# Scores a slot earlier, later turns of the second norms, reordered gathers and a split turning of the first keys in a fused language-model tower

## The chip, the cores and the metric

The kernel runs as one program on one core of a Trainium2 chip. Its time is the device time of one execution, in microseconds (us). The core has four engines that compute side by side, each with its own instruction stream: TensorE (PE in the profile; its weight loads are PEld), VectorE (DVE), ScalarE (ACT) and GpSimd (POOL). SyncE (SP) here only issues DMAs. The engines wait for one another by semaphores. The kernel before took 1109.43 us (median of three runs, 1108.84 to 1109.99).

## The reference

32 sequences of 128 tokens with 192 features, all in fp32, go through four steps:

```python
# 1 embedding
emb = word_table[ids] + domain_table[dom] @ proj_w.T + proj_b + types + pos
h = layer_norm(emb) * ln_gamma + ln_beta
# 2 "magnitude" attention, 12 heads of 16 features, on layer_norm(h)
sr = (qr @ kr.T + qi @ ki.T) * scale
si = (qi @ kr.T - qr @ ki.T) * scale
h = h + softmax(sqrt(sr * sr + si * si)) @ v
# 3 causal attention, 12 heads, on layer_norm(layer_norm(h)) (two norms, one behind the other)
x = layer_norm(h); x = x + attention(ln1(x)) @ proj_w + proj_b
# 4 mixture of 8 experts on ln2(x): the 2 best of 8 per token, at most 1280 tokens an expert
x = x + moe(ln2(x));  return h + x
```

## The kernel before

The 32 sequences are eight groups of four. Each group passes through the magnitude attention in one pass (passes 0 to 7) and through the causal attention in another (passes 8 to 15); the experts follow, from about 756 us on. A pass has 16 slots, and TensorE, VectorE, ScalarE and GpSimd walk the same passes and slots in their own `one_pass` functions. The work is software pipelined: while the group of the pass has its scores made, the group before has its probabilities transposed and multiplied by the values, and the next group has its input normalised, transposed and projected. What an engine does in a slot beside scores are "fills" (`fills_of`): pieces such as `xT` (transposes of the normalised input xn), `proj` and `value` (projections to q, k and values), `probT` (transposes of the probabilities), `ctx`, `ctxT`, `out`, `zT` and `logits`. Each fill takes the next of three places in PSUM in turn (`PLACE`, `RING`), so the order of the fills is the order in which the places come free.

*Magnitude scores.* A group has 12 jobs (four sequences x three blocks of heads), one a slot, job j in slot j + `SCORE_SLOT`. TensorE's `scores` multiplies k by q, both halves of the complex product from 32 rows of k: the second half uses `k_signed`, the keys with real and imaginary parts exchanged and one sign changed. ScalarE squares (`squares`), VectorE adds the squares and takes row maxima (`maxima`), ScalarE takes roots and later exponentials. The exchange is made by DMAs: VectorE writes k and k_signed of a block after its projection (in slots 12, 12 and 13 of the pass before), and SyncE copies k_signed in eight DMAs a block (sixteen partitions each) into k. The job of block b in a group's first three jobs waits for `keys_turned[b]`. In group 0 SyncE waits for all three blocks and issues eight DMAs that carry all of them (`first_turned`). For groups 1 to 7 that is 24 DMAs each, 168 in all.

*Embedding.* GpSimd gathers word, place (position and type) and domain rows by indirect DMAs, four of each a group (`gather_step`), and takes a power for the scale of each norm (`embedding_norm`: the first power in slot 4; the second in slot 6, or 12 for groups 2 to 7). VectorE makes xn from the second.

*Causal passes.* For each of a group's four sequences, three slots apart, come in turn `ctx` (values product done), `ctxT` (transposed context), `out` (output projection), `scale` (power on GpSimd), `norm` (VectorE makes z, the second norm's result), `zT` (TensorE transposes z), `keep` (z stored) and `logits` (router). `LAGS` gives the slots, counted from the group's own pass plus 16; the last group has shorter ones in `LAST_LAGS`.

*The set-up.* Before pass 0 SyncE also loads inputs and weights; the first groups have earlier projections (`EARLY_PROJ`).

Of the kernel before, what the change touches and what calls it, by code (L numbers as in the profile page):

```python
# [31 lines left out]
BLOCKS = 3  # L32
# [15 lines left out]
RING = 3  # L48
SCORE_SLOT = {"mag": 2, "cau": 3}
EXP_SLOT = 4  # L50
MAG_PROJ = (12, 12, 13, 13, 14, 15)
MAG_VALUE = (10, 14)
# [32 lines left out]

LAGS = {"ctx": 5, "ctxT": 7, "out": 9, "scale": 10, "norm": 12, "zT": 13, "keep": 13, "logits": 15}
LAST_LAGS = {"ctx": 5, "ctxT": 6, "out": 8, "scale": 8, "norm": 10, "zT": 11, "keep": 11, "logits": 13}
# [74 lines left out]
def tower_kernel(nc, ids, word_table, domain_cols, pos_table, kind_rows, domain_w, mag_qk, mag_v,  # L162
                 causal_qk, causal_qk_b, causal_v, ln_cols, rows, out_w, gate_w, fc_w, fc_b, pj_w, pj_b, out):
    ctx = ExitStack()
    with ctx:
# [6 lines left out]
        def sem(name):  # L172
            return ctx.enter_context(nc.semaphore(name))
# [161 lines left out]
        keys_signed = sem("keys_signed")  # L335
        first_turned = sem("first_turned")
        keys_turned = [sem(f"keys_turned{b}") for b in range(BLOCKS)]
        sign_made = sem("sign_made")
# [75 lines left out]
        CONST = 10 * 16  # L414
        
        blk = ctx.enter_context(nc.Block())

# [8 lines left out]
        def _(sp):  # L426
# [45 lines left out]
            sp.dma_start(fc_bias[:, :, :], fc_b).then_inc(bias_loaded, 16)  # L472

            sp.wait_ge(keys_signed, BLOCKS)
            for quarter, part in product(range(4), range(2)):
                to, of = 32 * quarter + HEAD_DIM * part, 32 * quarter + HEAD_DIM * (1 - part)
                sp.dma_start(k_of[0][to:to + HEAD_DIM, :, 1, :, :].rearrange("p b s k -> p b (s k)"),
                             k_signed[of:of + HEAD_DIM, :, :]).then_inc(first_turned, 16)
            for g in range(1, GROUPS):
# [62 lines left out]
        def _(pool):  # L542
# [69 lines left out]
            def embedding_norm(p, g, slot):  # L612
                first, second = (4, 6) if g < 2 else (4, 12)
                if slot == first:
                    pool.wait_ge(mag.named("emb_moments"), g + 1)
                    power(g, moments[:, :, 1], rstd[:, 0, :], WORD_EPS, mag, "emb_rstd")
                elif slot == second:
                    pool.wait_ge(mag.named("x_moments"), g + 1)
                    power(g, moments[:, :, 1], rstd[:, 1, :], LN_EPS, mag, "x_rstd")
# [121 lines left out]
        def _(pe):  # L741
# [112 lines left out]
            def scores(number, j):  # L854
# [7 lines left out]
                if p is mag and j % 3 == j:  # L862

                    if g > 0:
                        pe.wait_ge(keys_turned[j], 8 * 16 * g)
                    else:
                        pe.wait_ge(first_turned, 8 * 16)
                for pair in range(2):
# [30 lines left out]
            def one_pass(p):  # L899
                now, ready = group_of(p, 0), group_of(p, -1)  # L900
                for slot in range(STEPS):
# [4 lines left out]
                    if now is not None and 0 <= slot - SCORE_SLOT[phase_of(now)[0].name] < JOBS:  # L906
                        scores(now, slot - SCORE_SLOT[phase_of(now)[0].name])
                    if ready is not None and 1 <= slot <= JOBS:
                        values_product(ready, slot - 1)
                    for n, f in fills:  # L910
                        fill(n, f)

            def domain_products():
# [117 lines left out]
        def _(act):  # L1031
# [95 lines left out]
            def expert_weights_high(e, u):  # L1127
                act.wait_ge(raw_loaded, 48 * e + 48)
                apart(act)
                sc.activation(fc_hi[:, u, :, :], raw_fc, ACT.Copy).then_inc(fc_high, 1)  # L1130

            def first_weights_high(quarter):

# [4 lines left out]
            def one_pass(p):  # L1138
                now, ready = group_of(p, 0), group_of(p, -1)
                for slot in range(STEPS):  # L1140
# [12 lines left out]
                    for n, f in fills:  # L1153
                        fill(n, f)
                    if ready is not None and slot >= 3 and slot % 3 == 0 and slot // 3 <= GROUP:
                        copy_ctx(*phase_of(ready), slot // 3 - 1)
# [84 lines left out]
        def _(dve):  # L1241
# [12 lines left out]
            def fill(number, fl):  # L1254
# [35 lines left out]
                elif kind == "proj" and p is mag and s < 3:  # L1290
# [4 lines left out]
                    if g == 1:  # L1295
                        dve.wait_ge(first_turned, 8 * 16)
                    elif g > 1:
                        dve.wait_ge(keys_turned[s], 8 * 16 * (g - 1))
# [490 lines left out]
```

## Time and profile before

| what | value |
|---|---|
| median of the runs | 1109.43 us (1108.84 to 1109.99) |
| profiled execution, its own time | 1110.32 us |
| its span | 1107.4 us |
| busy share of the span | PE 86%, PEld 65%, ACT 61%, DVE 60%, POOL 41% |
| granted TensorE clock in 40 slices of 27.7 us, tenths | 7668889989999999999999998656999999999999 |
| mean of one squares instruction, L1101 (ScalarE) | 601 ns, x192 |
| mean of one maxima instruction, L1371 (VectorE) | 288 ns, x384 |
| granted clock, 59.5 to 61.0 us / 355.1 to 356.0 us | 0.50 / 1.00 |

A line such as `59.55 1.23 PE L877 MATMUL ... x8 [5.17 <-DMA k<-k_signed]` reads: at 59.55 us from the start of the span TensorE began eight matmuls of line 877, which took 1.23 us; it had stood idle for 5.17 us before, and the DMA named had released it. A name such as `ps_scores<-k,q` gives what is written and from what. `SPq` is SyncE's queue of DMA issues. Where TensorE waits, the whole pipeline moves back by that wait, unless a later piece has slack in another place.

### The profile page before, as it was taken

Reading aid. Unit: us, or ns where it says so; the run is one execution under the profiler, and the core shown is the slowest. Engines: PE = TensorE matmul, PEld = TensorE weight load, DVE = VectorE, ACT = ScalarE, POOL = GpSimd, SP = SyncE. Lnnn points to the kernel's source line nnn. Section 1 sums busy time; section 2 is a strip of 40 time slices with the busy share of each in tenths; the row PEclk is TensorE's granted clock in tenths of the full one; section 3 lists DMA queues with packets and bytes.
Section 4 is the critical chain, followed back from the end, with each engine's and each line's share of the span. In section 5 each row is a group of like instructions: output and inputs, shape, how many; then the busy total and the mean of one; then the engine's idle time right before and its main releaser. Section 6 shows DMA issues by size and latency. Waiting matters only on the chain.

```text
span 1107.4 us, 22074 instructions
## 1 busy us (share of the span) xinstructions
PE 947.6 (86%) x7209; PEld 724.2 (65%) x7210; DVE 666.7 (60%) x3063; ACT 676.9 (61%) x1438; POOL 458.7 (41%) x508
## 2 busy tenths in 40 slices
PE   2477778988988889999899989856999999999996
PEld 1444555565655566666666666545888888889896
DVE  1576778878988776767677665483443443443432
ACT  2148768958888978788778777354444443443431
POOL 7765547533110111222322122203667667567654
PEclk7668889989999999999999998656999999999999
DMA  7333223212011000011101101145454445564342
GB/s 212 66 50 59 45 54 72 38 41 47 13 24 48 13 2 1 2 35 35 34 2 35 35 18 48 34 85 70 74 106 84 79 104 79 76 111 78 50 52 28
DMA packets 63236, 59.24 MB, mean 53 GB/s; under 512 B 17278, under 2 KB 54176, under 8 KB 63136
## 3 DMA queue, kind: packets, MB, share of 16 engines
q0 software_dynamic: 25344, 27.89, 17.7%
q1 hardware_dynamic: 37792, 30.11, 10.6%
q8 instruction: 51, 0.84, 0.3%
q14 instruction: 49, 0.40, 0.1%
HBM read 35.28 MB, written 16.39 MB: 47 GB/s over the span
## 4 chain that ended last, share of the span: by engine, by line
PE 64%; DVE 14%; ACT 7%; issue 6%; POOL 3%; SPq 3%; DMA 2%; POOLq 0%; DVEq 0%; ACTq 0%
PE ps_scores L759 13%; PE ps_ring L751 11%; PE ps_ring L1003 9%; PE ps_ring L759 7%; PE ps_scores L877 5%; PE ps_ctx L894 5%; PE ps_scores L1003 4%; PE ps_scores L880 3%; SPq L484 2%; POOL got L573 2%; DVE probs L1377 2%; PE ps_ring L831 1%; PE ps_ring L830 1%; DMA k<-k_signed 1%; ACT square L1101 1%
## 5 line engine op out<-in xcount | busy, mean ns | idle before, releaser
L1214 ACT ACTIVATE probs<-ps_scores,fc_bias 128x512 f32<-128x512 f32 (+1 forms) x144 | 87.9, 616 | 148.6 <-PE ps_scores L759 143.7
L633 POOL DMA_INDIRECT out<-z_t,slots_now x80 | 135.2, 1690 | 103.6 <-DVE z_t L1688 73.8
L1092 ACT ACTIVATE prob_t<-ps_ring 128x512 f32<-128x512 f32 x192 | 114.1, 597 | 39.4 <-PE ps_ring L751 38.7
L751 PE MATMUL ps_ring<-ident,probs 128*128 128x128 f32 x768 | 127.8, 292 | 6.6 <-ACT k L1072 1.9
L1117 ACT ACTIVATE probs<-probs,neg_max 128x128 f32<-128x128 f32 x384 | 120.6, 395 | 3.5 <-DVE neg_max L1377 3.5
L1101 ACT ACTIVATE square<-ps_scores 128x512 f32<-128x512 f32 x192 | 104.8, 601 | 29.0 <-PE ps_scores L877 25.3
L1377 DVE CUSTOM_DVE_ANT_0 probs<-ps_scores,causal 128x128 f32<-128x128 f32 x384 | 88.8, 287 | 53.1 <-PE ps_scores L880 52.8
L1003 PE MATMUL ps_ring<-work,probs 128*128 128x192 f32 x672 | 115.9, 328 | 5.7 <-ACT probs L1214 5.4
L1003 PEld LDWEIGHTS ps_ring<-work,probs 128*128 128x128 f32 x672 | 109.2, 190 | 9.5 <-issue 9.5
L759 PE MATMUL ps_scores<-x_hi,fc_hi 128*128 128x512 f32 (+1 forms) x288 | 105.4, 372 | 7.3 <-DVE x_hi L1672 3.6
L1371 DVE CUSTOM_DVE_ANT_0 probs<-square 128x128 f32<-128x128 f32 x384 | 89.8, 288 | 35.3 <-ACT square L1101 32.0
L751 PEld LDWEIGHTS ps_ring<-ident,probs 128*128 128x128 f32 x768 | 91.9, 149 | 26.2 <-issue 12.7
L759 PE MATMUL ps_scores<-x_hi,fc_lo 128*128 128x512 f32 (+1 forms) x288 | 102.0, 360 | 0.0
L1669 DVE CAST x_hi<-x_full 128x512 fp32r<-128x512 f32 x40 | 18.2, 456 | 138.9 <-ACT x_full L1203 93.9
L877 PE MATMUL ps_scores<-k,q 32*128 32x256 f32 x768 | 92.3, 475 | 11.0 <-DMA k<-k_signed 5.6
L567 POOL TENSOR_SCALAR rstd<-moments 128x4 f32<-128x4 f32 x24 | 6.7, 281 | 212.0 <-DVE moments L1502 121.1
L759 PE MATMUL ps_ring<-x_hi,w_hi 128*128 128x512 f32 x160 | 71.8, 449 | 12.8 <-DVE k L1293 6.8
L567 POOL TENSOR_SCALAR rstd<-z_moments 128x1 f32<-128x1 f32 x32 | 7.3, 227 | 171.8 <-DVE z_moments L1335 171.8
L877 PEld LDWEIGHTS ps_scores<-k,q 32*128 32x128 f32 x768 | 45.8, 204 | 36.5 <-issue 24.6
L759 PEld LDWEIGHTS ps_scores<-x_hi,fc_hi 128*128 128x128 f32 x288 | 55.1, 191 | 18.7 <-issue 6.7
L759 PE MATMUL ps_ring<-x_hi,w_lo 128*128 128x512 f32 x160 | 65.5, 409 | 0.0
L751 PE MATMUL ps_ring<-ident,xn 128*128 128x128 f32 x160 | 29.5, 316 | 41.7 <-DVE xn L1438 31.8
(215 smaller groups left out, 2199.1 us busy)
## 6 DMA issues: line engine op xcount, KB each, us to landing
k<-k_signed SPq DMA_DIRECT2D x168, 32.0 KB
work<-pj_w SPq DMA_DIRECT2D x8, 576.0 KB
token_in<-xin SPq DMA_DIRECT2D x8, 384.0 KB, 3.4
out<-resid SPq DMA_DIRECT2D x8, 384.0 KB, 4.2
vals<-fc_w SPq DMA_DIRECT2D x8, 384.0 KB
vals<-fc_w SPq DMA_DIRECT2D x16, 192.0 KB
out<-z_t,slots_now POOLq DMA_INDIRECT x80
token_in<-xin SPq DMA_DIRECT2D x8, 128.0 KB, 4.4
```

The source lines that it names most:

```text
L633: gp.indirect_dma_start(out[:, :], bass.IndirectOffsetOnAxis(slots_now[:, u, 1, t:t + 1], 0), slot_y[:, o, :], None, compute_op=ALU.add).t ...
L751: return pe.transpose(dst, src, ident[0:n, 0:n])
L759: last = pe.matmul(dst, lhs, rhs, start=(k == 0), stop=(k == 4))
L877: last = pe.matmul(ps_scores[:, h, 0:256], q[r, b, s, :], k[r, b, :, s, :], start=True, stop=True)
L894: last = pe.matmul(ps_ctx[32 * h:32 * h + 32, 128 * b:128 * b + 128], vals_of[number % 2][:, s, 4 * b + h, :], prob_t[:, j % 2, h, :], sta ...
L1003: last = pe.matmul(ps_y[i][:, 0:HID], hidden[:, c % 2, f_, tok], pj_w_sb[:, u, f_, :], start=(f_ == 0), stop=(f_ == FF_CHUNKS - 1))
L1092: sc.activation(prob_t[:, s % 2, :, :], src.rearrange("p (h q) -> p h q", h=4), ACT.Exp if p is mag else ACT.Copy).then_inc(ring_free[i], 1)
L1101: sc.activation(square[:, j % 2, h, :, :].rearrange("p h m k -> p h (m k)"), ps_scores[:, h, 0:256], ACT.Square).then_inc(mag.scores_free, 1)
L1117: last = sc.activation(probs[:, j, h, :], probs[:, j, h, :], ACT.Exp, bias=neg_max[:, s, 4 * b + h:4 * b + h + 1], scale=-1.0)
L1214: sc.activation(hidden[:, c % 2, f_, 0:128 * nt], ps_scores[:, i, 0:128 * nt], ACT.Gelu, bias=fc_bias[:, e, f_:f_ + 1]).then_inc(gelu_done ...
L1371: last = ve.tensor_tensor_reduce(out=probs[:, j, h, :], in0=square[:, j % 2, h, 0, :], in1=square[:, j % 2, h, 1, :], scale=1.0, scalar=-3 ...
L1377: last = ve.tensor_tensor_reduce(out=probs[:, j, h, :], in0=ps_scores[:, h, 0:128], in1=causal[:, :], scale=-(HEAD_DIM ** -0.5), scalar=3. ...
```

## The change

It has five parts. The scores of a magnitude pass start in slot 1 in place of 2 (`SCORE_SLOT`), so the jobs stand in slots 1 to 12. In the causal passes, but for the last group, `zT`, `keep` and `logits` come one slot later. GpSimd's first power of groups 2 to 7 stands in slot 8 of the embedding's slots and no longer in 4, with that behind the gathers of place rows. The first keys are turned in two steps: SyncE turns block 0 as soon as it is signed, then blocks 1 and 2 are turned by four DMAs of SyncE and four of ScalarE. And the values product of slot 1 comes after that slot's fills.

```diff
-SCORE_SLOT = {"mag": 2, "cau": 3}
+SCORE_SLOT = {"mag": 1, "cau": 3}
 EXP_SLOT = 4
+FIRST_Q = 3
...
-LAGS = {"ctx": 5, "ctxT": 7, "out": 9, "scale": 10, "norm": 12, "zT": 13, "keep": 13, "logits": 15}
+LAGS = {"ctx": 5, "ctxT": 7, "out": 9, "scale": 10, "norm": 12, "zT": 14, "keep": 14, "logits": 16}
...
+        def turn_first_keys(eng, quarter, part, b, done):
+
+            to, of = 32 * quarter + HEAD_DIM * part, 32 * quarter + HEAD_DIM * (1 - part)
+            eng.dma_start(k_of[0][to:to + HEAD_DIM, b, 1, :, :].rearrange("p b s k -> p b (s k)"),
+                          k_signed[of:of + HEAD_DIM, b, :]).then_inc(done, 16)
...
+            sp.wait_ge(keys_signed, 1)
+            for quarter, part in product(range(4), range(2)):
+                turn_first_keys(sp, quarter, part, slice(0, 1), first_turned)
             sp.wait_ge(keys_signed, BLOCKS)
-            for quarter, part in product(range(4), range(2)):
-                to, of = 32 * quarter + HEAD_DIM * part, 32 * quarter + HEAD_DIM * (1 - part)
-                sp.dma_start(k_of[0][to:to + HEAD_DIM, :, 1, :, :].rearrange("p b s k -> p b (s k)"),
-                             k_signed[of:of + HEAD_DIM, :, :]).then_inc(first_turned, 16)
+            for quarter, part in product(range(2), range(2)):
+                turn_first_keys(sp, quarter, part, slice(1, BLOCKS), rest_turned)
...
-                first, second = (4, 6) if g < 2 else (4, 12)
+                first, second = (4, 6) if g < 2 else (8, 12)
...
-                        pe.wait_ge(first_turned, 8 * 16)
+                        pe.wait_ge(first_turned if j == 0 else rest_turned, 8 * 16)
...
-                    if ready is not None and 1 <= slot <= JOBS:
+                    turned = ready is not None and ready < GROUPS and slot == 1
+                    if ready is not None and 1 <= slot <= JOBS and not turned:
                         values_product(ready, slot - 1)
                     for n, f in fills:
                         fill(n, f)
+                    if turned:
+                        values_product(ready, slot - 1)
...
+            def turn_rest_of_keys():
+
+                act.wait_ge(keys_signed, BLOCKS)
+                for quarter, part in product(range(2, 4), range(2)):
+                    turn_first_keys(act, quarter, part, slice(1, BLOCKS), rest_turned)
...
                     for n, f in fills:
                         fill(n, f)
+                        if (n, f) == (0, ("proj", FIRST_Q)):
+                            turn_rest_of_keys()
...
-                        dve.wait_ge(first_turned, 8 * 16)
+                        dve.wait_ge(first_turned if s == 0 else rest_turned, 8 * 16)
```

The order of the instructions follows from these numbers. TensorE at the start of a magnitude pass (pass 5; `ident,probs` are probability transposes of the group before, `ident,xn` input transposes of the next, `k,q` scores, `prob_t,vals` the values product), before:

```order
L751 MATMUL ps_ring<-ident,probs 128x128 x4
L751 MATMUL ps_ring<-ident,xn 128x128 x4
L751 MATMUL ps_ring<-ident,probs 128x128 x4
L894 MATMUL ps_ctx<-prob_t,vals 32x128 x4
L751 MATMUL ps_ring<-ident,xn 128x128 x4
L751 MATMUL ps_ring<-ident,probs 128x128 x4
L877 MATMUL ps_scores<-k,q 128x256 x4
L894 MATMUL ps_ctx<-prob_t,vals 32x128 x4
```

The same place on TensorE after the change:

```order
L760 MATMUL ps_ring<-ident,probs 128x128 x4
L760 MATMUL ps_ring<-ident,xn 128x128 x4
L760 MATMUL ps_ring<-ident,probs 128x128 x4
L886 MATMUL ps_scores<-k,q 128x256 x4
L760 MATMUL ps_ring<-ident,xn 128x128 x4
L903 MATMUL ps_ctx<-prob_t,vals 32x128 x4
L760 MATMUL ps_ring<-ident,probs 128x128 x4
L886 MATMUL ps_scores<-k,q 128x256 x4
```

The first scores moved from slot 2 to slot 1, ahead of the second input transposes, and the first values product behind these.

GpSimd in the pass in which group 2 is embedded (`got` are the gathered rows, `rstd<-moments` and `rstd<-rstd,half` one power), before:

```order
L573 DMA got<-word_table,id_now 128x192 x4
L567 TENSOR_SCALAR rstd<-moments 128x4
L569 TENSOR_TENSOR rstd<-rstd,half 128x4
L573 DMA got<-place_rows,id_now 128x192 x4
L573 DMA got<-domain_rows,id_now 128x192 x4
L567 TENSOR_SCALAR rstd<-moments 128x4
L569 TENSOR_TENSOR rstd<-rstd,half 128x4
```

The same place on GpSimd after:

```order
L582 DMA got<-word_table,id_now 128x192 x4
L582 DMA got<-place_rows,id_now 128x192 x4
L576 TENSOR_SCALAR rstd<-moments 128x4
L578 TENSOR_TENSOR rstd<-rstd,half 128x4
L582 DMA got<-domain_rows,id_now 128x192 x4
L576 TENSOR_SCALAR rstd<-moments 128x4
L578 TENSOR_TENSOR rstd<-rstd,half 128x4
```

The first power moved behind the four place gathers; between the two powers stand now four gathers and not eight.

TensorE at the start of a causal pass (`ident,z` is `zT`, `g_w,z_t` `logits`, `o_w,work` `out`), before:

```order
L751 MATMUL ps_ring<-ident,probs 128x128 x4
L751 MATMUL ps_ring<-ident,ctx_n 128x128
L751 MATMUL ps_ring<-ident,ctx_n 64x128
L751 MATMUL ps_ring<-ident,z 128x128
L751 MATMUL ps_ring<-ident,z 64x128
L751 MATMUL ps_ring<-ident,probs 128x128 x4
L894 MATMUL ps_ctx<-prob_t,work 32x128 x4
L751 MATMUL ps_ring<-ident,xn 128x128 x4
```

The same place on TensorE after:

```order
L760 MATMUL ps_ring<-ident,probs 128x128 x4
L760 MATMUL ps_ring<-ident,ctx_n 128x128
L760 MATMUL ps_ring<-ident,ctx_n 64x128
L849 MATMUL ps_ring<-g_w,z_t 128x8
L850 MATMUL ps_ring<-g_w,z_t 128x8
L760 MATMUL ps_ring<-ident,probs 128x128 x4
L903 MATMUL ps_ctx<-prob_t,work 32x128 x4
L760 MATMUL ps_ring<-ident,z 128x128
L760 MATMUL ps_ring<-ident,z 64x128
L760 MATMUL ps_ring<-ident,xn 128x128 x4
```

The transposes of z moved one slot on, behind the next probability transposes and values product, and the logits of the sequence before into the slot that they left.

## Rows read from the trace of the kernel before

**Rows 1.** the page's chain by engine; TensorE's waits: us in total, times, longest us

```profile
PE 64%; DVE 14%; ACT 7%; issue 6%; POOL 3%; SPq 3%; DMA 2%; POOLq 0%; DVEq 0%; ACTq 0%
PE ps_ring L751 <- DVE z L1352: 15.4, 21, 1.1
```

**Rows 2.** timeline of 45 to 63 us (start, us taken, [idle before <-releaser]); third row: chain

```profile
45.84 0.62 DVE L1299 TENSOR_SCALAR k_signed<-k,sign 128x512 f32<-128x512 f32 x1
50.20 5.24 SPq L477 DMA_DIRECT2D k<-k_signed  x8
54.84 4.43 DMA k<-k_signed
59.55 1.23 PE L877 MATMUL ps_scores<-k,q 32*128 32x256 f32 x8 [5.17 <-DMA k<-k_signed]
61.61 1.62 PE L877 MATMUL ps_scores<-k,q 32*128 32x256 f32 x8 [0.82 <-ACT square L1101]
```

**Rows 3.** timeline, xn in passes 1 and 4, GpSimd's gathers of pass 4

```profile
117.29 1.09 PE L751 MATMUL ps_ring<-ident,xn 128*128 128x128 f32 x4 [4.21 <-DVE xn L1438]
202.39 1.67 POOL L573 DMA_INDIRECT got<-place_rows,id_now  x1 [0.20 <-issue]
217.97 1.55 POOL L573 DMA_INDIRECT got<-domain_rows,id_now  x1 [0.30 <-issue]
221.04 0.67 DVE L1432 TENSOR_SCALAR xn<-resid,moments,rstd 128x192 f32<-128x192 f32 x2 [4.14 <-POOL rstd L569]
```

**Rows 4.** SyncE's key DMAs, TensorE's scores (passes 2, 4, 5, 7); last two: chain

```profile
134.79 15.37 SPq L484 DMA_DIRECT2D k<-k_signed  x24
215.76 15.19 SPq L484 DMA_DIRECT2D k<-k_signed  x24
263.82 15.06 SPq L484 DMA_DIRECT2D k<-k_signed  x24
339.31 15.31 SPq L484 DMA_DIRECT2D k<-k_signed  x24
149.45 1.06 PE L877 MATMUL ps_scores<-k,q 32*128 32x256 f32 x8
153.18 0.71 PE L877 MATMUL ps_scores<-k,q 32*128 32x256 f32 x8 [1.29 <-issue]
236.15 1.06 PE L877 MATMUL ps_scores<-k,q 32*128 32x256 f32 x8
278.81 1.06 PE L877 MATMUL ps_scores<-k,q 32*128 32x256 f32 x8
280.74 0.71 PE L877 MATMUL ps_scores<-k,q 32*128 32x256 f32 x8
355.20 0.71 PE L877 MATMUL ps_scores<-k,q 32*128 32x256 f32 x8
357.34 0.71 PE L877 MATMUL ps_scores<-k,q 32*128 32x256 f32 x8 [0.48 <-DMA k<-k_signed]
149.56 2.54 DMA k<-k_signed
354.03 3.26 DMA k<-k_signed
```

**Rows 5.** timeline of TensorE, end of pass 5

```profile
307.93 0.50 PE L759 MATMUL ps_ring<-x_hi,w_hi 128*128 128x512 f32 x1 [1.24 <-DVE ctx_n L1316]
```

**Rows 6.** causal pass, TensorE's waits; windows (us, PE PEld DVE ACT POOL busy, clock, DMA)

```profile
551.18 0.42 PE L894 MATMUL ps_ctx<-prob_t,work 128*32 128x128 f32 x8 [0.44 <-ACT ctx_t L1124]
566.68 0.41 PE L751 MATMUL ps_ring<-ident,z 128*128 128x128 f32 x2 [0.66 <-DVE z L1352]
572.79 0.41 PE L751 MATMUL ps_ring<-ident,z 128*128 128x128 f32 x2 [0.67 <-DVE z L1352]
579.72 0.41 PE L751 MATMUL ps_ring<-ident,z 128*128 128x128 f32 x2 [0.86 <-DVE z L1352]
504.82:543.39 38.57, 35.80 (x350) 25.59 (x349) 27.50 (x169) 30.85 (x84) 9.72 (x22) 1.00 0.10 26
```

More of the change, by code:

```diff
@@ L336, in tower_kernel @@
         first_turned = sem("first_turned")
+        rest_turned = sem("rest_turned")
         keys_turned = [sem(f"keys_turned{b}") for b in range(BLOCKS)]
```

## The prediction

> **What bounds the kernel now.** I read the chain that ended last first, then TensorE's waits, then three stretches of the timeline. In the chain TensorE has 64%, VectorE 14%, ScalarE 7%, SyncE's queue 3% and DMAs 2% [rows 1]. So a change pays where TensorE stands still. The reader is to see three kinds of such places. Before pass 0 TensorE waits 5.17 us for the turned keys: SyncE issues eight DMAs from 50.20 on (5.24 us), the last lands at 59.27 (54.84 + 4.43), although block 0 was signed at 46.46 [rows 2]. In pass 1 it waits 4.21 us for xn, and in pass 4 VectorE waits 4.14 us ahead of xn and TensorE behind it, because GpSimd gave the second scale only after eight gathers [rows 3]. In a causal pass it waits 0.66, 0.67 and 0.86 us for z, and 0.44 for a copy of the context [rows 6]; over the kernel z costs 15.4 us in 21 waits [rows 1].
>
> I also looked for what is late but hidden. It is the turning of the keys in the later magnitude passes: 24 DMAs by SyncE alone take 15.06 to 15.37 us from the first signed block on [rows 4], and then they land: at 152.10 (149.56 + 2.54) for pass 2 and at 357.29 (354.03 + 3.26) for pass 7 [rows 4]. Counted from SyncE's first issue that is 17.3 and 18.0 us. In pass 5 the job that needs the last block (job 2) starts at 280.74 without a wait, 16.9 us after the first issue [rows 4], so the DMAs needed no more than that. In pass 7 the same job did wait, 0.48 us [rows 4]. This path is full already, and the change asks for it one slot earlier.
>
> **The change part by part.** The sum is made against the profiled execution, 1110.32 us (span 1107.4); the median of the runs shown is 1109.43, 0.9 lower.
>
> *First keys.* SyncE now starts at 46.46, eight DMAs of one block. Eight took 5.24 us (0.65 each), so they end near 51.7; a set of one block is taken to land about 2 us later, and its bounds are 1.4 and the 3.84 us that the set of all blocks needed after its last issue (55.43 to 59.27). The last q is copied by ScalarE after its own four issues (4 x 0.65 = 2.6 us, ahead of two q and two value copies), so job 0 can start near 55.0 in place of 59.55. The other two blocks are eight DMAs by two queues, SyncE's ending near 54.3, landing near 57, so job 1 starts near 57 in place of 61.61 [rows 2]. One more job now stands ahead of the first transposes of the next group, 2.05 us of the 4.5 (59.55 to 61.61 is one job's step). Net 2.7 us at the projections (bounds 0.5 and 4.5). Then ScalarE's tail of pass 0 is the path, and it has one pair of squares less in it, 1.1 us (2 x 601 ns by the page's mean, with some overlap). Together -3.8 us.
>
> The Trainium skill, DMA: Bandwidth & Descriptors, Issuing engines are not separate DMA queues, says that DMAs from several engines share the same 16 engines, and that a second issuer saves issue time only. If it is the transfer and not the issue that sets the landing here, the last block still lands at 59.27, job 1 starts there, and 2.2 us of this part are lost.
>
> *Gathers around the powers, passes 1 to 7 on GpSimd.* The four place gathers now come ahead of the first power. In pass 4 GpSimd stood idle before that power, since VectorE's moments are late; it ran the first place gather from 202.39 on and the last domain gather from 217.97 to 219.52, 17.1 us for eight; the second power stood behind them, and VectorE 4.14 us behind the power [rows 3]. Half of those 17.1 us, the place gathers and their landing, go into the idle time, so the domain gathers end some 8 us sooner where 4.14 are wanted: the wait goes, and VectorE's own work is next. What it costs is that the first power comes behind the gathers; the affine step that needs it is two slots further on, and only in pass 1 do I expect VectorE to wait (1 to 2 us, made good before slot 7). Worth 4.2 in pass 1 [rows 3]. Pass 4 is below, since the keys cut it.
>
> *Slots 1 to 12.* Job j now stands a slot earlier in each magnitude pass. This takes four maxima out of the crowded end of a pass (four of 288 ns by the page's mean, which overlap in part; some 0.9 us), behind which k, xn and ctx_n and so TensorE wait (1.24 us at 307.93, then for prob_t) [rows 5]; and job 0 now runs in that second wait. By TensorE alone a pass would gain 0.9 to 1.5 us. But job 2 needs block 2 in slot 3 and not 4. From SyncE's first issue to TensorE's scores in slot 3 it is now 149.45 - 134.79 = 14.7 us in pass 2, 20.4 in pass 4, 15.0 in pass 5, 15.9 in pass 7 [rows 4]; passes 3 and 6, whose rows look alike, have 16.9 and 16.1. The keys want 17.3, 16.9, 16.9 and 18.0 there, and 16.9 and 17.3 in passes 3 and 6. From that slot on to the next signed key there are ten jobs after as before, so the difference is a loss or a gain whole: pass 2 +2.6, against which its old wait in slot 4 (1.29 at 153.18 [rows 4]) and part of what TensorE lost behind it go: 0; pass 3: 0; pass 4: -3.5 (its old stall of 4.14 and what TensorE lost behind it go, cut at the keys' landing); pass 5 +1.9, pass 6 +1.2, pass 7 +2.1. The end of pass 7 has no keys and gives 1.0. Sum -3.5 + 5.2 - 1.0 = +0.7 us. Bounds: the keys cost nothing (-5.2 of it), or each transfer takes a microsecond longer (+5).
>
> *Values product after the fills in slot 1.* It waits for prob_t anyway; 0, bounds -0.3 and +0.3 a pass.
>
> *Second norms' turns.* z is made in the slot before its transpose; out, sum, statistics and z run on VectorE one behind the other. With one slot more (a sixteenth of a causal pass of 38.57 us [rows 6], 2.4) all three waits are covered: 2.19 us a pass, groups 0 to 5 and part of 6 of the causal ones; the last group keeps its lags. ScalarE's two copies of z move to slots 4 and 7, where a q copy and exponentials stand; 0.7 us more there, 0.7 less in slots 3 and 6, which helps the 0.44. I take 2.0 a pass, six passes: -12. Bounds: 2.6 x 6 = -15.6 if the context's wait goes too, and -5 if ScalarE in slots 4 to 8 becomes late. What is next then is VectorE in slots 9 to 13.
>
> Sum: -3.8 - 4.2 + 0.7 - 12 = -19.3. 1110.3 - 19.3 = 1091.0 for a profiled execution, 1090 as a median.
>
> **The rivals.**
> *A, the keys never bind.* Their landing is quicker than the chain shows, or the passes are paced by VectorE; then passes 2 to 7 gain 0.9 each and the key losses of 5.2 go: 1090 - 5.2 - 3 = 1082. For it: in pass 5 the keys had landed by 280.74, how long before isn't shown. Against: the chain goes through them in passes 2 and 7.
> *B, the causal passes get a new wait.* ScalarE is busy 30.85 of 38.57 us of a causal pass [rows 6] and its longest slots get longer; of 12 us 5 stay: 1097. Against: VectorE makes z, so ScalarE isn't what it waits for, and the other 7.7 us of a pass are free.
> *C, slower.* TensorE stands still for the keys in slot 3 of each of passes 2 to 7, and its clock falls behind each wait. Eight score matmuls take 1.23 us where the granted clock is 0.50, 1.2 GHz (59.55), and 0.71 where it is 1.00, 2.4 GHz (355.20) [rows 2, 4]; some 7 us of work at the low level cost 3.5 a pass. Six passes make 21; the keys' own 5.2 are in the sum already: 1090 + 21 = 1111. It decides from 19 us on, 3.2 a pass. Against: TensorE already waits about 3 us at the end of pass 5 (1.24 of it in [rows 5]), and the page's granted clock is 9 tenths or more in all slices from 10 to 24, 249 to 664 us.
> The Trainium skill, TensorE: Matmul & The Clock Gate, HAM oscillation — how this bites in real kernels, describes this pattern: a DMA wait in each turn of a loop puts the clock back to half each time. The granted clock just named does not show it yet, with waits about as long once a pass; by that rule and these rows the time would be C's 1111.
> *D, the change in the order is absorbed*: none of the waits named is on the path, 1109. The chain contains z and the keys, so little for it.
>
> **How the numbers follow.** The forecast has 0.55, A 0.15, B 0.20, C 0.04, D 0.06. The time is the forecast's, 1090. A run of this kernel tells 0.2% (2.2 us) from no change. The range must leave out 2 in 10: it reaches down to A, 1082, and up past B to 1100. Faster: forecast, A, B and a little of D, 0.92; same 0.04; slower 0.04.
>
> **What would show it.** Right: job 0 of pass 0 near 55 us and job 1 near 57; no wait over 1 us for xn in passes 1 and 4; in magnitude passes 2, 5, 6 and 7 a wait of job 2 for the turned keys, 1 to 3 us each, SyncE's 24 issues still taking 15 us; no TensorE wait for z but in the last group; a causal pass of 36.4 to 36.8 us in place of 38.57. Wrong: no wait for keys (A), a wait for prob_t or ctx_t over 1 us in slots 5 to 9 of a causal pass (B), a granted clock of half in the middle of several magnitude passes (C).

## The result and the profile after

The changed kernel takes 1100.26 us (median of 20 runs, 1093.61 to 1110.46), the kernel before 1109.88 us beside it (20 runs, 1105.19 to 1116.05); the ratio is 0.9915, with a 95% interval of 0.9889 to 0.9941. So it is 9.4 us faster by the ratio (6.5 to 12.3), where 19.3 were forecast, and 1100.26 lies just above the range of 1082 to 1100. Single runs of one kernel differ by 1 to 1.5% here, so that the 0.2% named in the prediction can't be told by a few runs. The profiled execution took 1102.23 us, its span is 1100.3. The views below are of that one execution.

The page of the changed kernel, the chain by engine, and three sums of TensorE's waits (total us, times, longest):

```profile
PE 68%; DVE 9%; SPq 8%; issue 5%; ACT 5%; DMA 2%; POOL 2%; another core or an unknown queue 1%; POOLq 0%; DVEq 0%; ACTq 0%
PE ps_ring L760 <- DVE z L1372: 1.4, 2, 0.7
PE ps_scores L886 <- DMA k<-k_signed: 18.5, 7, 3.8
PE ps_ctx L903 <- ACT prob_t L1104: 6.5, 5, 1.9
```

Against [rows 1], the waits for z went from 15.4 to 1.4 us, and SyncE's queue rose in the chain from 3% to 8%: there are now 18.5 us of waits for keys. Where they are, in TensorE's timeline (start, us taken, idle before). The first row is job 0 of pass 0, the second job 1; the others are job 2 in slot 3 of passes 2 to 7. The seventh wait of the sum, 0.56 us, is that of job 1 in pass 7.

```profile
54.31 0.71 PE L886 MATMUL ps_scores<-k,q 32*128 32x256 f32 x8
58.40 1.62 PE L886 MATMUL ps_scores<-k,q 32*128 32x256 f32 x8 [3.37 <-ACT square L1113]
148.80 1.06 PE L886 MATMUL ps_scores<-k,q 32*128 32x256 f32 x8 [3.85 <-DMA k<-k_signed]
188.91 0.71 PE L886 MATMUL ps_scores<-k,q 32*128 32x256 f32 x8 [1.37 <-DMA k<-k_signed]
228.29 1.24 PE L886 MATMUL ps_scores<-k,q 32*128 32x256 f32 x8 [3.57 <-DMA k<-k_signed]
275.87 1.24 PE L886 MATMUL ps_scores<-k,q 32*128 32x256 f32 x8 [2.32 <-DMA k<-k_signed]
316.81 1.24 PE L886 MATMUL ps_scores<-k,q 32*128 32x256 f32 x8 [2.99 <-DMA k<-k_signed]
358.77 1.23 PE L886 MATMUL ps_scores<-k,q 32*128 32x256 f32 x8 [3.79 <-DMA k<-k_signed]
```

None of the passes is spared, and behind four of the six waits the eight matmuls take 1.23 or 1.24 us, the time that they have at half clock, in place of 0.71. Behind a fifth, that of pass 2, the clock falls just after job 2: a window of the four microseconds behind that wait (us; busy and count of PE, PEld, DVE, ACT, POOL; granted clock; DMA share; GB/s) has 0.57, and only behind the shortest, 1.37 us in pass 3, does it stay at 1.00.

```profile
148.80:152.80 4.00, 4.00 (x32) 2.49 (x32) 1.57 (x10) 2.36 (x5) 1.94 (x2) 0.57 0.11 33
```

The SyncE rows of the same kernel, for passes 2 to 7 (start, us for 24 issues):

```profile
130.80 16.43 SPq L493 DMA_DIRECT2D k<-k_signed  x24
172.37 15.04 SPq L493 DMA_DIRECT2D k<-k_signed  x24
210.63 16.26 SPq L493 DMA_DIRECT2D k<-k_signed  x24
259.43 15.04 SPq L493 DMA_DIRECT2D k<-k_signed  x24
299.70 15.69 SPq L493 DMA_DIRECT2D k<-k_signed  x24
341.23 16.10 SPq L493 DMA_DIRECT2D k<-k_signed  x24
```

They answer to [rows 4]. In the kernel before, passes 2 to 7 have 15.37, 15.08, 15.19, 15.06, 16.12 and 15.31 us; passes 2, 4 and 7 are now 0.8 to 1.1 us longer, the other three as long or shorter.

The table lays the span out by the end of each group's first signed key, then by the first scores of each causal pass. "7" reaches to the first causal scores; "tail" is pass 15, the last context and the experts. Each column is one profiled execution; that of score_undone is 5.2 us below the median of its runs, that of half_keys 4.2 above, so a difference of a few microseconds between columns need not be one between kernels.

| stretch (us) | before | changed | score_undone | half_keys | busy_wait |
|---|---|---|---|---|---|
| to first key | 46.5 | 46.4 | 46.6 | 47.4 | 46.5 |
| 0 | 33.5 | 32.5 | 29.5 | 31.6 | 32.0 |
| 1 | 54.8 | 52.0 | 49.8 | 48.0 | 51.9 |
| 2 | 42.3 | 41.6 | 38.2 | 39.7 | 41.9 |
| 3 | 38.7 | 38.3 | 39.2 | 36.9 | 39.0 |
| 4 | 48.1 | 48.8 | 43.7 | 39.1 | 43.0 |
| 5 | 36.8 | 40.3 | 36.8 | 35.8 | 38.7 |
| 6 | 38.7 | 41.5 | 37.6 | 36.4 | 39.4 |
| 7 | 54.1 | 56.5 | 53.5 | 51.2 | 56.3 |
| 8 to 14 | 261.0 | 254.1 | 254.7 | 261.5 | 254.5 |
| tail | 453.0 | 448.5 | 445.8 | 445.9 | 446.1 |

From before to changed: 1.0 and 2.8 us gained in passes 0 and 1, 8.3 us lost in passes 2 to 7 (-0.7, -0.4, +0.7, +3.5, +2.8, +2.4), 6.9 gained in passes 8 to 14 and 4.5 in the tail.

### The profile page after: what moved, and what is told of

It reads as the page before. It is cut to its first block, busy times and chain, and to the rows that moved or that the text cites. A ratio compares the mean times of both kernels' runs of the same rounds, so it can differ in the third digit from the quotient of the medians.

```text
span 1100.3 us, 22081 instructions
## 1 busy us (share of the span) xinstructions
PE 954.1 (87%) x7209; PEld 729.7 (66%) x7210; DVE 669.5 (61%) x3063; ACT 675.9 (61%) x1438; POOL 461.8 (42%) x508
## 3 DMA queue, kind: packets, MB, share of 16 engines
q0 software_dynamic: 25344, 27.89, 17.9%
## 4 chain that ended last, share of the span: by engine, by line
PE 68%; DVE 9%; SPq 8%; issue 5%; ACT 5%; DMA 2%; POOL 2%; another core or an unknown queue 1%; POOLq 0%; DVEq 0%; ACTq 0%
PE ps_scores L768 13%; PE ps_ring L760 13%; PE ps_ring L1015 9%; SPq L493 8%; PE ps_ring L768 7%; PE ps_scores L886 6%; PE ps_ctx L903 6%; PE ps_scores L889 4%; PE ps_scores L1015 4%; PE ps_ring L840 1%; PE ps_ring L839 1%; DMA k<-k_signed 1%; DVE probs L1397 1%; ACT probs L1122 1%; ACT square L1113 1%
## 5 line engine op out<-in xcount | busy, mean ns | idle before, releaser
L1104 ACT ACTIVATE prob_t<-ps_ring 128x512 f32<-128x512 f32 x192 | 114.3, 598 | 39.3 <-PE ps_ring L760 37.6
L760 PE MATMUL ps_ring<-ident,probs 128*128 128x128 f32 x768 | 132.3, 300 | 3.3 <-DVE x_hi L1288 1.3
L1391 DVE CUSTOM_DVE_ANT_0 probs<-square 128x128 f32<-128x128 f32 x384 | 89.7, 287 | 49.1 <-ACT square L1113 39.2
L1397 DVE CUSTOM_DVE_ANT_0 probs<-ps_scores,causal 128x128 f32<-128x128 f32 x384 | 88.6, 286 | 46.6 <-PE ps_scores L889 46.3
L886 PE MATMUL ps_scores<-k,q 32*128 32x256 f32 x768 | 94.5, 501 | 23.5 <-DMA k<-k_signed 18.5
L760 PEld LDWEIGHTS ps_ring<-ident,probs 128*128 128x128 f32 x768 | 94.6, 153 | 23.3 <-issue 13.1
L886 PEld LDWEIGHTS ps_scores<-k,q 32*128 32x128 f32 x768 | 46.4, 217 | 48.5 <-DMA k<-k_signed 20.1
```

The costliest lines, as they stand in the source:

```text
L760: return pe.transpose(dst, src, ident[0:n, 0:n])
L886: last = pe.matmul(ps_scores[:, h, 0:256], q[r, b, s, :], k[r, b, :, s, :], start=True, stop=True)
L1104: sc.activation(prob_t[:, s % 2, :, :], src.rearrange("p (h q) -> p h q", h=4), ACT.Exp if p is mag else ACT.Copy).then_inc(ring_free[i], 1)
L1391: last = ve.tensor_tensor_reduce(out=probs[:, j, h, :], in0=square[:, j % 2, h, 0, :], in1=square[:, j % 2, h, 1, :], scale=1.0, scalar=-3 ...
L1397: last = ve.tensor_tensor_reduce(out=probs[:, j, h, :], in0=ps_scores[:, h, 0:128], in1=causal[:, :], scale=-(HEAD_DIM ** -0.5), scalar=3. ...
```

## The experiments

Each ratio is to the kernel before, timed in the same session, with its 95% interval. Lengths of passes and waits are each from one profiled execution.

### One part at a time

**score_undone**: `SCORE_SLOT = {"mag": 1, ...}` back to `{"mag": 2, ...}` in the changed kernel.

> The changed kernel with the scores back in slots 2 to 13, the other four parts kept. Theory K: no wait for keys over 0.6 us is left, passes 5 to 7 get their old lengths back (36.8, 38.7 and 54.1 us from signed key to signed key), 8.6 us, less what the earlier slots gave in passes 2 and 3 (about 1): 7 us faster than the changed kernel, a ratio to the kernel before of 0.985. Rival P: as the changed kernel, 0.991.

Measured: 1082.45 us, ratio 0.9775 (0.9740 to 0.9809). The four other parts are worth 25 us; the earlier slot takes 15 of them away (11 to 20 by the two intervals). It was meant to give back 7. Waits for keys of 2.4, 1.4 and 1.1 us are left in passes 0, 2 and 4, where the expectation had none over 0.6.

**score_alone**: the kernel before with that number alone changed from 2 to 1.

> The kernel before with the magnitude scores in slots 1 to 12 and nothing else changed. Theory K (the keys): job 2 now meets the turned keys in slot 3, TensorE waits for them in each of passes 2 to 7, 2 to 4 us each except pass 3 and 4 (which still have their old stall for xn), and the clock falls behind the wait; 12 us lost against some 7 gained by the earlier jobs, so +5 us, a ratio of 1.004. Rival P (pace: the passes are set by ScalarE's and VectorE's work, and the waits for keys only take the place of others): no change, 1.000.

Measured: 1116.34 us, ratio 1.0075 (1.0046 to 1.0104): slower, by 8.3 us. TensorE waits 17.7 us for keys, of which 5.1 are the old wait of pass 0 and 12.7 stand in passes 2 to 7; the changed kernel has 18.5 there. The same edit costs 8 us alone and 15 with the others. Pass 4 shows why: here TensorE still needs 19.6 us from SyncE's first issue to slot 3, and the keys don't bind; in the changed kernel it needs 14.1 and then waits 3.57.

**lags_alone**: `"zT": 13, "keep": 13, "logits": 15` to `14, 14, 16` in the kernel before.

> The kernel before with zT, keep and logits one slot later and nothing else changed. Theory Z (the prediction's step): the 15.4 us of waits for z shrink to 1.4 and the causal passes give back 2 us each, 10 to 12 us in all, a ratio of 0.990. Rival: in the changed kernel passes 10 and 11 stayed at 38.5 and 38.3 us with a clock of 0.96 where 38.9 and 38.6 us stood before, so the gain is only 7 us, 0.9937, and some pass of 9 to 14 stays over 38 us here too.

Measured: 1099.95 us, ratio 0.9868 (0.9827 to 0.9909), 14.6 us; the waits for z shrink from 15.4 to 0.5 us. In its profiled execution the tail is 7.5 us shorter and passes 8 to 14 only 1.8, with passes of 38.3 to 40 us among them, as the rival had it.

**power_alone**: `(4, 12)` to `(8, 12)` in the kernel before.

> The kernel before with GpSimd's first power of groups 2 to 7 in slot 8, behind the place gathers, and nothing else changed. If the step is worth what the changed kernel with its scores back in slots 2 to 13 shows (passes 1, 2 and 4 shorter by 5.0, 4.1 and 4.3 us), 12 us faster, 0.989. If it is worth what the prediction gave it (4.2 in pass 1, 3.5 in pass 4), 7.7 us, 0.993.

Measured: 1101.23 us, ratio 0.9902 (0.9865 to 0.9939), 10.9 us, passes 1, 2 and 4 shorter by 2.1, 2.3 and 4.8 us.

**first_alone**: `turn_first_keys` and `rest_turned` in the kernel before.

> The kernel before with the first keys turned in two steps by two queues and nothing else changed. The prediction's step: pass 0, from 46.5 us to group 1's first signed key, 3.8 us shorter than 33.5; ratio 0.9965. Rival: the changed kernel's 32.5 us is what the step gives, 1.0 us, 0.999, since ScalarE stands idle 3.4 us ahead of its second value copy.

Measured: 1107.25 us, ratio 0.9957 (0.9932 to 0.9982), 4.8 us, pass 0 30.6 us long, with an idle time of ScalarE of 3.4 us in it.

**values_back**: the changed kernel with

```diff
-                    turned = ready is not None and ready < GROUPS and slot == 1
+                    turned = False
```

> The changed kernel with the values product of slot 1 ahead of the fills again, as in the kernel before. The prediction put this part at 0 (-0.3 to +0.3 us a pass): 0.9915 again. Rival: with the first scores in slot 1 the product would wait for prob_t ahead of the input transposes, 1.25 us in each of six passes as in the kernel before, unless the keys' wait takes it in: 0.998.

Measured: 1102.35 us, ratio 0.9933 (0.9902 to 0.9964). Its interval holds the changed kernel's 0.9915, so this part can't be told from nothing. The waits for prob_t do grow, from 6.5 to 10.7 us, and those for keys shrink from 18.5 to 17.3.

### Are the keys the cause

**half_keys**, for groups 2 to 7 of the changed kernel:

```diff
-                    for quarter, part in product(range(4), range(2)):
+                    for quarter, part in product(range(4), range(2 if g < 2 else 1)):
...
-                                     k_signed[of:of + HEAD_DIM, b, :]).then_inc(keys_turned[b], 16)
+                                     k_signed[of:of + HEAD_DIM, b, :]).then_inc(keys_turned[b], 16 if g < 2 else 32)
```

> The changed kernel that leaves out every second key DMA of groups 2 to 7 (their second halves are not turned), so that SyncE needs 7.5 and not 15 us a group. Theory K: no wait for keys from pass 2 on (18.4 us in seven waits in the changed kernel), of which 3 to 5 us come back as waits for prob_t; with the clock that falls behind them 14 to 16 us faster than the changed kernel, a ratio to the kernel before of 0.978. Rival P: ScalarE is busy 33 of 37 to 41 us in these passes, so most of the waits turn into waits for prob_t and the gain is 3 us at most, 0.989.

Measured: 1070.85 us, ratio 0.9665 (0.9637 to 0.9693), lower than both theories had it. One wait for keys is left, in pass 0. The keys cost the changed kernel 2.5%, 28 us: more than their 18.5 us of waits. In the table passes 2 to 7 are some 28 us shorter than the changed kernel's; passes 8 to 14 are 7.4 longer, which nothing here explains. And against score_undone (0.9775) the earlier scores are worth 12 us where the keys don't hold them up. TensorE's waits in half_keys:

```profile
PE ps_scores L886 <- DMA k<-k_signed: 2.0, 1, 2.0
PE ps_ctx L903 <- ACT prob_t L1104: 6.9, 5, 1.9
```

The waits for prob_t have hardly grown, so the rival by which the pace of ScalarE takes the gain back has fallen.

**early_proj**: `MAG_PROJ = (12, 12, 13, 13, 14, 15)` to `(10, 11, 12, 13, 14, 15)` in the changed kernel; the three key projections, and so the first turning, two slots earlier.

> The changed kernel with the three key projections of groups 2 to 7 in slots 10, 11 and 12 in place of 12, 12 and 13, so that the turning starts two slots (4.5 us) earlier. Theory K: as half_keys, the waits of 1.4 to 3.9 us for keys go, 0.978 to 0.982 against the kernel before. Rival P: 0.989 to 0.993, and the waits for prob_t grow by as much as those for keys shrink.

Measured: 1074.62 us, ratio 0.9703 (0.9672 to 0.9735), lower than both theories had it, with no wait for keys but one of 1.4 us in pass 0.

**undone_early**: the same edit in score_undone.

> The changed kernel with its scores back in slots 2 to 13 and the key projections of groups 2 to 7 in slots 10, 11 and 12. Theory K: the keys did not bind with the scores in slot 2 but for 1.4 and 1.1 us in passes 2 and 4, so the earlier projections add those 2.5 us at most: 0.975 against the kernel before, and the early scores with early projections (0.970) stay the better pair. Rival R: what early_proj gained over the kernel with its scores put back came from the earlier projections and not from the slot of the scores; then 0.968 or less.

Measured: 1091.82 us, ratio 0.9821 (0.9782 to 0.9860). Rival R is out, and theory K's 0.975 was too low. Earlier projections don't help by themselves: with the scores in slot 2 nothing comes of them (5 us slower, which the intervals of score_undone and undone_early don't separate), with the scores in slot 1 they give 23.

**early_11**: `(11, 11, 12, 13, 14, 15)` in the changed kernel.

> The changed kernel with the key projections of groups 2 to 7 in slots 11, 11 and 12, one slot earlier than 12, 12 and 13; between the changed kernel (0.9915) and early_proj (0.9703). Theory K: the turning starts some 2.3 us earlier, so waits of 3.85, 1.37, 3.57, 2.32, 2.99 and 3.79 us in passes 2 to 7 become 1.6, 0, 1.3, 0, 0.7 and 1.5; the 1.72 us waits for ctx_t that early_proj has in six passes do not come; 1074 us, 0.970 again (0.966 to 0.976). Rival: it is the clock more than the length of a wait that costs, and with waits of about 1.5 us left it still falls; 0.980.

Measured: 1086.36 us, ratio 0.9790 (0.9747 to 0.9833), with 6.6 us of waits for keys: 2.35 in pass 2, 2.33 in pass 4, 1.48 in pass 6 and two of 0.2. Here theory K's number was too low; the rival's 0.980 fits. In the four microseconds from the start of job 2 on the granted clock is 0.50 in pass 2 and 0.70 in pass 4, and 1.00 behind the 1.48. The waits for ctx_t came all the same, 10.5 us in six; what these are worth is seen below, in spread_proj. Three doses of one cause: 18.5 us of waits 0.9915, 6.6 us 0.9790, 1.4 us 0.9703.

### Issue or transfer

**two_queues**: in the changed kernel SyncE turns three quarters of the partitions and ScalarE the fourth:

```diff
-                    for quarter, part in product(range(4), range(2)):
+                    for quarter, part in product(range(3), range(2)):
...
+                        if 1 <= n < GROUPS and f[0] == "proj" and f[1] >= FIRST_Q:
+                            b = f[1] - FIRST_Q
+                            act.wait_ge(keys_signed, BLOCKS * n + b + 1)
+                            for part in range(2):
+                                to, of = 96 + HEAD_DIM * part, 96 + HEAD_DIM * (1 - part)
+                                act.dma_start(k_of[n % 2][to:to + HEAD_DIM, b, 1, :, :]..., k_signed[of:of + HEAD_DIM, b, :]).then_inc(keys_turned[b], 16)
```

> The changed kernel with six key DMAs a block by SyncE and two by ScalarE's queue, behind its q copies. Theory K with issue as the limit: SyncE's 18 issues take 11.5 us and not 15.3, the waits for keys shrink by up to 3.8 us each and all but vanish, ScalarE pays 6 x 0.65 = 3.9 us a pass in slots 13 to 15 where its roots stand; net 0.980 against the kernel before (0.974 to 0.988). Rival: the transfers and not the issues limit (the 16 DMA engines are shared), then the waits stay at 2 to 4 us and ScalarE's time comes on top: 0.995 or more.

Measured: 1082.76 us, ratio 0.9775 (0.9735 to 0.9816). Pass 5's keys in its timeline, SyncE's 18 and ScalarE's first four issues:

```profile
251.26 11.34 SPq L493 DMA_DIRECT2D k<-k_signed  x18
253.51 0.51 ACTq L1180 DMA_DIRECT2D k<-k_signed  x1
254.06 0.62 ACTq L1180 DMA_DIRECT2D k<-k_signed  x1
255.41 1.16 ACTq L1180 DMA_DIRECT2D k<-k_signed  x2
```

The same bytes on the same DMA engines, and the waits for keys are gone. So the limit is the issue, 0.63 us each in a row on one queue, and not the bytes. The Trainium skill, DMA: Bandwidth & Descriptors, Issuing engines are not separate DMA queues, says that a second issuer saves only the time to initiate, and the trace agrees; it adds that this is usually small beside the DMA itself, and here it is the larger part.

### The clock behind a wait

**busy_wait**: TensorE does eight matmuls of no use ahead of the wait for keys:

```diff
+                if p is mag and j == 2 and g >= 2:
+                    pe.wait_ge(p.scores_free, 2 * (JOBS * g + j) + 1)
+                    for _ in range(8):
+                        pe.matmul(ps_scores[:, 0, 0:128], ident[:, :], ident[:, :], start=True, stop=True)
                 if p is mag and j % 3 == j:
```

> The changed kernel in which TensorE does eight matmuls of no use (128x128, about 2.4 us) ahead of the wait of job 2 for the turned keys, in groups 2 to 7, so that it is busy for most of a wait. Theory C (the clock): besides the waits (18.4 us) the changed kernel loses 6 to 9 us because the granted clock falls to half behind them; with TensorE busy the keys land as late, but job 2's eight matmuls take 0.71 us and not 1.24 in passes 4 to 6, the granted clock from 46.5 to 400 us is 0.90 or more in place of 0.87, and the time falls by 5 us, 0.987. Rival W: only the waits cost; the time stays at 0.9915, or grows by the 1 us by which the matmuls outlast the wait in pass 3.

Measured: 1091.43 us, ratio 0.9868 (0.9844 to 0.9892), 5.2 us faster than the changed kernel by the ratios, with more work in it; by the two intervals the gain is 1 to 9 us. By chance pass 4's keys land at the same microsecond in both profiles. busy_wait's rows, the useless matmuls (each is recorded as two) and the scores:

```profile
225.29 2.02 PE L874 MATMUL ps_scores<-ident 128*128 128x128 f32 x16
228.29 0.71 PE L890 MATMUL ps_scores<-k,q 32*128 32x256 f32 x8 [0.99 <-DMA k<-k_signed]
```

The 8 us behind that landing, by windows (us; busy and count of PE, PEld, DVE, ACT, POOL; granted clock; DMA share; GB/s), in busy_wait:

```profile
228.29:236.30 8.01, 8.01 (x88) 5.26 (x88) 6.02 (x37) 6.58 (x13) 1.35 (x2) 1.00 0.01 3
```

and in the changed kernel:

```profile
228.30:236.30 8.00, 8.00 (x59) 4.23 (x60) 4.65 (x27) 4.83 (x9) 0.00 (x0) 0.50 0.00 1
```

TensorE is busy throughout in both. At 1.2 GHz (0.50) it gets through 59 matmuls, at 2.4 GHz (1.00) through 88. The stretch from this pass's first signed key to the next takes 48.8 us in the changed kernel and 43.0 in busy_wait. It is the pass with the largest difference: 5.8 of the 8.7 us between the two executions in passes 2 to 7. The clock was not held everywhere: 3.2 us of wait are left behind the useless matmuls of pass 2, and in pass 7 a wait of 1.3 us came ahead of job 1, before them; at both places the clock falls. From 46.5 to 400 us, the kernel before, the changed kernel and busy_wait:

```profile
46.50:400.00 353.50, 298.24 (x2475) 197.98 (x2475) 277.75 (x1316) 266.58 (x461) 133.66 (x122) 0.90 0.23 42
```

```profile
46.50:400.00 353.50, 299.65 (x2436) 197.68 (x2434) 274.55 (x1295) 263.88 (x455) 135.28 (x121) 0.87 0.23 42
```

```profile
46.50:400.00 353.50, 311.64 (x2610) 212.11 (x2608) 280.64 (x1337) 269.10 (x472) 138.41 (x127) 0.91 0.23 42
```

The Trainium skill, TensorE: Matmul & The Clock Gate, HAM oscillation — how this bites in real kernels, tells of a loop whose DMA wait puts the clock back in each turn. The trace agrees in passes 2 and 4 to 7 of the changed kernel, with a wait of 2.3 to 3.9 us once a pass, and not in pass 3, where the wait is 1.4.

### A better version

**spread_proj**: `MAG_PROJ = (10, 12, 13, 13, 14, 15)` in the changed kernel.

> The changed kernel with the key projections of groups 2 to 7 in slots 10, 12 and 13 (early_proj had 10, 11 and 12). Theory K: what matters is when SyncE's 24 issues begin, not where the last block is signed, since its own eight need 5 us and 1.4 to land; so the waits for keys stay away as in early_proj, and with two projections in slot 13 again the wait of 1.72 us for ctx_t that early_proj has at the end of each of passes 2 to 7 goes: 0.962 to 0.966. Rival: the 1.72 us are ScalarE's pace at the end of a pass and come back under another name: 0.970.

Measured: 1074.14 us, ratio 0.9693 (0.9673 to 0.9714). No wait for keys is left: with the last block signed where it always was, an earlier start of the issues is enough. The wait for ctx_t fell, from early_proj's row

```profile
PE ps_ring L760 <- ACT ctx_t L1136: 12.2, 7, 1.9
```

to spread_proj's

```profile
PE ps_ring L760 <- ACT ctx_t L1136: 1.9, 1, 1.9
```

but the time did not: the ratios are 0.9703 and 0.9693. The rival's 0.970 was right; where those 10 us went was not looked for. Both versions beat the kernel before by 3% and the changed kernel by 2.2%; which of the two is better these runs don't tell.

## Why the prediction was wrong

- **First keys, -3.8 us: the turning held, the earlier slot in pass 0 was priced too low.** first_alone gave 4.8 us of time and 2.9 in pass 0; in score_undone pass 0 is 4.0 shorter. Job 0 ran at 54.31, near the 55.0 forecast. In the changed kernel only 1.0 us came, with job 1 at 58.40 and not at 57. The term had a net cost of 1.0 for the job that now stands ahead of the transposes (2.05 less 1.1). score_alone, with the old turning, has 1.7 (pass 0 is 35.2 us long and not 33.5). The rest goes with an idle time of ScalarE ahead of its second value copy:

```profile
57.27 0.49 ACT L1090 ACTIVATE vals<-ps_ring 128x384 f32<-128x384 f32 x1 [3.44 <-remote]
```

  It is not the whole loss, for first_alone and undone_early have it too (3.39 and 3.37 us), with pass 0 at 30.6 and 30.4 us against 29.5 in score_undone, which has 0.58. With the scores in slot 1, pass 0 takes 32.5 us with it in the changed kernel, and 30.5 (early_proj) and 31.6 (half_keys) with 0.58. So the idle time costs some 1 to 2 us and the slot as much again. What ScalarE waited for there isn't known. A slip of the sum is small beside this: 4.5 less 2.05 is 2.5 at the projections, and not 2.7.
- **Gathers, -4.2 in pass 1 and -3.5 in pass 4: right in sum, too large in pass 1.** power_alone took 10.9 us off, of them 2.1 in pass 1. The wait of 4.21 us for xn in pass 1 [rows 3] is gone; in its place stand 2.80 us at the same transposes, for x_hi:

```profile
116.07 1.11 PE L760 MATMUL ps_ring<-ident,xn 128*128 128x128 f32 x4 [2.80 <-DVE x_hi L1288]
```

  In pass 4 VectorE no longer waits for the second scale. The gain in pass 2 I had not seen.
- **Second norms, -12 us: right in sum.** 6.9 us came in passes 8 to 14, 4.5 in the tail, and lags_alone measured 14.6 (10 to 19). The place was off: I had put all of it in six passes, 2.0 each. Passes 12 to 14 gave 1.4, 1.7 and 2.7, pass 9 gave 1.5, passes 10 and 11 0.3 each, and pass 8 took 0.9 us more. Windows of pass 12 and of pass 11 in the changed kernel:

```profile
542.48:579.70 37.22, 35.85 (x350) 25.96 (x349) 28.02 (x167) 30.70 (x84) 9.74 (x22) 1.00 0.09 27
504.17:542.48 38.31, 37.36 (x350) 26.93 (x349) 27.60 (x167) 30.70 (x84) 9.89 (x22) 0.96 0.09 26
```

  A granted clock of 0.96 goes with the 1.1 us more; the kernel before had 1.00 in its pass [rows 6]. A pass of 38 to 40 us of this kind appears in most kernels with the later lags, in different passes, and in two_queues in none; why the clock falls there was not tried.
- **Slots 1 to 12, +0.7 us: this step failed.** Passes 2 to 7 lost 8.3 us, and, with the other parts in place, the earlier slot costs 15 us and not the 4.2 that I had (the +5.2 of the keys less the 1.0 of the last pass), or 5.2 with pass 0. The step had two sides. The keys' side was right. I took 17.3, 16.9, 16.9, 16.9, 17.3 and 18.0 us from the first issue to job 2, 103.3 in all; the rows above give 18.0, 16.5, 17.7, 16.4, 17.1 and 17.5, 103.3 in all before rounding. TensorE's side was wrong, and this is what failed. I read its way from the first issue to slot 3 off the kernel before: 14.7, 16.9, 20.4, 15.0, 16.1 and 15.9. With the wait taken out, it needed 14.2, 15.2, 14.1, 14.1, 14.1 and 13.8 (18.00 - 3.85 in pass 2, and so on). In all that is 99.0 us before and 85.4 after. Of the difference 5.3 us are time in which TensorE was busy, 74.3 us before and 69.0 after, with a granted clock of 0.83 to 1.00 before and 0.91 to 1.00 after; the other 8.2 are mostly waits that the change itself removed or shortened: 4.4 us for k in pass 4, behind the late xn, and waits of 1.2 to 3.2 us for prob_t in five of the six passes, of which at most 1.9 is left. The loss by keys is what is left once they are gone. So the six waits are 17.9 us in place of some 8, in each pass and not in four of them.
- **The clock.** I gave rival C, the clock behind each wait, 4 in 100, and took nothing of it into the forecast. The argument against it, a clock of 9 tenths from 249 us on in the kernel before, was about 3 us a pass in pieces of 1.2; the new waits are 1.4 to 3.9 in one piece. The clock does fall, behind the five of them that are 2.3 us or longer, and TensorE then works at 0.50 for 3.4 us in pass 2, 9.5 in pass 4, 6.3 in passes 5 and 6 and 5.3 in pass 7 (from windows of half a microsecond), where C had 7. But its price is about 5 us by busy_wait and not C's 21. The kernel before had a granted clock of 0.90 from 46.5 to 400 us, and its own falls there go into the comparison; the changed kernel has 0.87. The 28 us by half_keys (24 to 32) are then 18 of waits and about 5 of clock (1 to 9); some 5 stay open, and part of them can be clock too, since busy_wait did not hold it everywhere.
- **The rivals.** A (keys never bind, 1082) had the right size for what the earlier slots are worth without the keys: half_keys is 12 us ahead of score_undone and early_proj 8, where A had 8. Its own sum is loose: six passes at 0.9 make 5.4, and it takes 3. B (a new wait in the causal passes, 1097) came nearer to the time, but not by its cause: no wait for prob_t or ctx_t over 1 us stands in slots 5 to 9 of a causal pass, and the loss is in passes 2 to 7. D fell with the first row on z.
- **The signs** to look for were named rightly: job 0 near 55, SyncE's issues 15 us long, a wait of job 2 in passes 2, 5, 6 and 7, a causal pass of 36.4 to 36.8 us (36.9 in pass 13). The numbers beside them (1 to 3 us) were too small in passes 2 and 7, and passes 3 and 4 had such a wait too.

## What to carry to other kernels

When a change takes waits out of a loop and also moves a consumer earlier, price the consumer's new wait against the loop with its waits gone, not against the old distances: a producer that is just on time today will be late by all that the loop gains. Look at what the producer is made of before moving the consumer; here 24 DMA issues in a row, at 0.63 us each, ran on one queue, and starting them two slots earlier, a change of one number in spread_proj, turned a gain of 0.9% into one of 3%. And the waits of 2.3 to 3.9 us of TensorE cost more than their length here: look at the granted clock in the window behind a wait, and count only what the kernel before did not lose already.

## What was not expected of the hardware

- The issue of a key DMA takes nearly the same time for one, two or three blocks: 24 of 16x512 took 15.04 us, 0.63 each, and eight of 16x3x512 5.24 us, 0.66 each [rows 2]. Twelve in a row, of which four carry twice as much, took 7.65 us in the changed kernel:

```profile
46.38 7.65 SPq L421 DMA_DIRECT2D k<-k_signed  x12
```

- Half the clock did not halve the matmuls done: 59 against 88 records, of mixed shapes, in 8 us with TensorE busy in both, a ratio of 0.67.
- Eight matmuls of no use in each of six passes, 2 us each (3.4 at half clock in pass 7), made the kernel 5 us faster (1 to 9).
